# A four-layer network on one core: dense experts 512 wide, linear attention and the last stage in another order, routing and Exp in groups

## Time and profile before

| | before |
|---|---|
| time, median of 3 runs (range) | 5162.6 us (5162.58 to 5174.09) |
| the profiled execution's own time | 5173.64 us |
| its span | 5171.9 us |
| granted TensorE clock, mean | 0.946 |
| TensorE busy | 4497.5 us (87%), 36266 matmuls |
| VectorE busy | 3763.9 us (73%) |
| ScalarE busy | 3222.1 us (62%) |
| GpSimd busy | 2164.2 us (42%) |

### The profile page before, as it was taken

How to read it: one execution, slowest core, us unless ns; L and a number is a source line. 1 busy time by engine, 2 the same in 40 slices (tenths; PEclk the granted TensorE clock), 3 DMA queues, 4 the chain that set the end, 5 groups by cost and what they waited for, 6 DMA issues and landing times. The chain is left out here.

```text
span 5171.9 us, 91179 instructions
## 1 busy us (share of the span) xinstructions
PE 4497.5 (87%) x36266; PEld 2367.1 (46%) x36266; DVE 3763.9 (73%) x4573; ACT 3222.1 (62%) x4306; POOL 2164.2 (42%) x1131
## 2 busy tenths in 40 slices
PE   6999999999987998677878699868859988899998
PEld 3666666666755443111111244356634443333333
DVE  6888888888644776598898377757757756787777
ACT  3777777777833775377777477745527754444544
POOL 3888888888800232000000022234412224566665
PEclk7999999999998999599999799989979998999999
DMA  2111211111101110100000111000011103333333
GB/s 59 39 39 42 45 41 39 39 39 39 26 3 39 45 61 23 42 21 29 17 25 9 43 62 55 28 18 1 1 43 48 55 30 82 85 93 90 95 95 78
DMA packets 83156, 227.89 MB, mean 44 GB/s; under 512 B 18708, under 2 KB 23988, under 8 KB 79092
## 3 DMA queue, kind: packets, MB, share of 16 engines
q1 hardware_dynamic: 82767, 222.49, 15.4%
HBM read 160.12 MB, written 11.98 MB: 33 GB/s over the span
## 5 line engine op out<-in xcount | busy, mean ns | idle before, releaser
L527 POOL TENSOR_TENSOR a_prob_low<-a_prob_whole,a_prob_high 128x1024 f16<-128x1024 f32 x512 | 1084.8, 2131 | 276.8 <-ACT a_prob_high L417 276.8
L2263 DVE TENSOR_TENSOR e_low<-e_whole,e_high 128x1024 f16<-128x1024 f32 x400 | 696.5, 1763 | 284.5 <-ACT e_high L2221 284.5
L501 DVE TENSOR_REDUCE a_part_max<-a_top 128x2 f32<-128x1024 f32 x512 | 626.3, 1223 | 218.3 <-PE a_top L328 212.4
L414 ACT ACTIVATE a_prob_whole<-a_score 128x1024 f32<-128x1024 f32 x512 | 525.0, 1025 | 332.6 <-PE a_score L317 320.6
L778 ACT ACTIVATE a_prob<-a_score 128x512 f32<-128x512 f32 x1024 | 532.9, 604 | 259.4 <-PE a_score L722 259.4
L811 DVE TENSOR_REDUCE a_part_max<-a_side 128x2 f32<-128x1024 f32 x512 | 595.7, 1221 | 88.4 <-PE a_side L693 88.4
L2246 POOL TENSOR_TENSOR all_res_t<-all_res_t,e_gated 128x1024 f32<-128x1024 f32 x100 | 239.0, 2390 | 816.8 <-DVE e_gated L2272 816.8
L2218 ACT ACTIVATE e_whole<-e_hidden,e_bias 128x1024 f32<-128x1024 f32 x400 | 445.1, 1113 | 217.6 <-PE e_hidden L2169 130.7
L1920 POOL TENSOR_TENSOR m_scaled<-m_acted,m_gate 128x512 f32<-128x512 f32 x264 | 432.1, 1640 | 343.4 <-DVE m_acted L2047 255.9
L417 ACT ACTIVATE a_prob_high<-a_score 128x1024 f16<-128x1024 f32 x512 | 522.3, 1020 | 0.0
L316 PE MATMUL a_score<-a_qa,a_ka 128*128 128x256 f16 x2048 | 476.3, 273 | 0.0
(11 more groups left out here) (333 smaller groups left out, 10279.6 us busy)
## 6 DMA issues: line engine op xcount, KB each, us to landing
m_gate<-gates SPq DMA_DIRECT2D x264, 256.0 KB, 5.1
e_gate<-gates SPq DMA_DIRECT2D x25, 2048.0 KB, 7.2
a_ka<-a_nat_high_k SPq DMA_DIRECT2D x128, 128.0 KB, 2.4
e_w<-in_w_moe SPq DMA_DIRECT2D x25, 512.0 KB, 7.7
a_qa<-a_nat_high_q SPq DMA_DIRECT2D x64, 128.0 KB, 2.4
a_qa<-a_nat_low_q SPq DMA_DIRECT2D x64, 128.0 KB, 2.4
a_qb<-a_nat_high_q SPq DMA_DIRECT2D x64, 128.0 KB, 2.4
a_kb<-a_nat_low_k SPq DMA_DIRECT2D x64, 128.0 KB, 2.4
```

Of the source, the lines that this page charges most:

```text
L414: eng.activation(prob_whole[:, e % RING, :, :, :], score[:, e % 2, :, :, :], ACT.Exp, scale=scale)
L501: eng.tensor_reduce(part_max[:, i, c, :, qt % 4], top[:, :, :], AX.X, ALU.max).then_inc(max_done, 1)
L527: eng.tensor_tensor(prob_low[:, e % RING, :, :, :], prob_whole[:, e % RING, :, :, :], prob_high[:, e % RING, :, :, :], ALU.subtract).then_ ...
L2263: eng.tensor_tensor(low[:, s % HR, :], whole[:, s % 2, :], high[:, s % HR, :], ALU.subtract).then_inc(low_done, 1)
```

## The change

- Dense experts: W from 1024 to 512, so 32 steps a unit, a product of three matmuls, four hidden and four output banks (HB, OB), LAG 4, HR 8, SPLIT_AT 12: the same data in flight. ScalarE's, VectorE's and GpSimd's operations become 512 wide.
- Rope attention: the projections of batch 1 alone move 13 events ahead.
- Linear attention: another ORDER, for all engines.
- Last stage: START 24 to 12, PERIOD 35 to 34. VectorE and GpSimd take a step's part of it one slot later (UP_LAG 1), high and lows at HIGH_LAG 2 as before, the output at LAG 4; VectorE's addition is first in the slot after, mixing jobs last. ScalarE does high before Silu. The Exp jobs are split in two groups, slots 10 and 13; Sqrt from 45 to 36. Constants are padded with zeros to 128x128 tiles, and the pick matmuls accumulate. Routing is one chain per group of eight tiles, `weights(g)`; transposes go through `out` and `o_ps` in slots 2 to 5, ScalarE copies them, four stores with their own semaphores. The low half of x is made by GpSimd.

```diff
-                put(start + 1, "q", b + 1)
-                put(start + 3, "k", b + 1)
-                put(start + 9, "v", b + 1)
+                early = EV - 3 if b == 0 else 0
+                put(start + 1 - early, "q", b + 1)
+                put(start + 3 - early, "k", b + 1)
+                put(start + 9 - early, "v", b + 1)
...
-    ORDER = [("k0", 0), ("v0", 0), ("q0", 0), ("state", 1), ("ksum", 1), ("k1", 0), ("turn0", 2), ("v1", 0), ("fold", 1),
+    ORDER = [("k0", 0), ("state", 1), ("v0", 0), ("ksum", 1), ("q0", 0), ("turn0", 2), ("k1", 0), ("fold", 1), ("v1", 0),
              ("turn1", 2), ("q1", 0), ("out0", 2), ("out1", 2)]
...
-    PART_LAG, LAG, SPLIT_AT = 2, 4, 8
+    UP_LAG, HIGH_LAG, LAG, SPLIT_AT = 1, 2, 4, 8
     HB, AR, SR, HR = 2, 3, 4, 6
-    START, PERIOD = 24, 35
-    SLOTS = START + STEPS + LAG
+    START, PERIOD = 12, 34
+    SLOTS = START + STEPS + LAG + 1
     PAIR = 2 * BANK
-    GROUP_TILES = BANK // SMALL_EXPERTS
+    GROUP_TILES = PAIR // P
     BANKS = NT // GROUP_TILES
-    ROUTED = 1 + 2 * BANKS + 5
+    CHAIN = 7
...
-             "w0": 9, "w1": 9, "w2": 10, "w3": 10, "v0": 11, "k0": 12, "r0": 13, "v1": 14, "k1": 15, "r1": 16, "o0": 17,
-             "v2": 18, "k2": 19, "r2": 20, "o1": 21, "v3": 22, "k3": 23, "r3": 24, "o2": 25, "g": 26, "o3": 27,
+             "w0": 8, "w1": 9, "v0": 10, "w2": 11, "w3": 12, "k0": 13, "r0": 14, "v1": 15, "k1": 16, "r1": 17, "o0": 18,
+             "v2": 19, "k2": 20, "r2": 21, "o1": 22, "v3": 23, "k3": 24, "r3": 25, "o2": 26, "g": 27, "o3": 28,
              "mean": 30, "var": 33, "out": 63}
-    ACT_AT = {"low": 1, "low5": 2, "wt": 6, "ew0": 10, "ew1": 10, "ew2": 10, "ew3": 10,
-              "decay0": 10, "decay1": 10, "decay2": 10, "decay3": 10, "vs0": 12, "vs1": 15, "vs2": 19, "vs3": 23,
-              "gs": 27, "o": 28, "sq": 32, "std": 45}
+    ACT_AT = {"low": 1, "low5": 2, "wt": 6, "ew0": 10, "ew1": 10, "decay0": 10, "decay1": 10, "vs0": 11,
+              "ew2": 13, "ew3": 13, "decay2": 13, "decay3": 13, "vs1": 16, "vs2": 20, "vs3": 24,
+              "gs": 28, "o": 29, "sq": 32, "std": 36}
     DVE_AT = {"z": -1, "mixed1": 3, "mixed3": 4, "mixed2": 5, "mixed0": 7, "mixed4": 8,
-              "kv0": 13, "carry0": 13, "scan0": 13, "u0": 14, "rs0": 14, "kv1": 16, "carry1": 16, "scan1": 16, "u1": 17, "rs1": 17,
-              "kv2": 20, "carry2": 20, "scan2": 20, "u2": 21, "rs2": 21, "kv3": 24, "carry3": 24, "scan3": 24, "u3": 25, "rs3": 25,
-              "cen": 31, "eps": 34, "rstd": 47, "norm": 50, "affine": 50, "gated": 53, "res": 64}
+              "kv0": 14, "carry0": 14, "scan0": 14, "u0": 15, "rs0": 15, "kv1": 17, "carry1": 17, "scan1": 17, "u1": 18, "rs1": 18,
+              "kv2": 21, "carry2": 21, "scan2": 21, "u2": 22, "rs2": 22, "kv3": 25, "carry3": 25, "scan3": 25, "u3": 26, "rs3": 26,
+              "cen": 31, "eps": 34, "rstd": 43, "norm": 45, "affine": 45, "gated": 47, "res": 64}
     POOL_AT = {"delta": -2, "x1": 3, "x3": 4, "x2": 5, "x0": 7, "x4": 8}
-    LAST = {"std": 35, "rstd": 35, "norm": 36, "affine": 36, "gated": 36, "out": 37, "res": 38}
+    LAST = {"std": 35, "rstd": 36, "norm": 36, "affine": 36, "gated": 36, "out": 38, "res": 39}
...
+        shape = {"cols": [P, 20], "w_x1": [P, 2, P], "w_x2": [P, 5, P], "w_w1": [P, P], "w_w2": [P, GROUPS, P], "w_r": [P, GROUPS, P], "w_k": [P, GROUPS, P], "w_v": [P, GROUPS, P],
+                 "w_g": [P, P], "w_o": [P, P], "pick": [P, GROUPS, P], "blocks": [P, P]}
...
-                eng.wait_ge(turned_free, CH)
-                eng.dma_start(gates_d, gates_t[:, :]).then_inc(stored, 16)
-                eng.wait_ge(stored, 16)
+
+                def store(pair):
+                    eng.wait_ge(copied, 2 * (pair + 1))
+                    eng.dma_start(gates_d[:, pair * PAIR:(pair + 1) * PAIR], gates_t[:, pair % 2, :]).then_inc(stored[pair], 16)
+
+                for pair in range(2):
+                    store(pair)
                 for n in range(UNITS):
                     for pair in range(CH // 2):
                         g = n * (CH // 2) + pair
+                        if n == 0:
+                            eng.wait_ge(stored[pair], 16)
+                        if g == 1:
+                            store(2)
+                            store(3)
...
+                    eng.wait_ge(found, 1 + CHAIN * (g + 1))
+                    if i >= 2:
+                        eng.wait_ge(copied, i - 1)
                     for t in range(4):
-                        mm = eng.transpose(turned[0:EX, t * P:(t + 1) * P], gates[:, 4 * c + t, :], ident[:, :])
+                        mm = eng.transpose(turned[i % 2][0:EX, t * P:(t + 1) * P], gates[:, g % 2, i % 2 * 4 + t, :], ident[:, :])
                     mm.then_inc(turned_full, 1)
...
-                        eng.matmul(o_ps[32 * j:32 * j + 32, :], const["pick"][:, :], rs[:, j % 2, :], start=True, stop=True).then_inc(pe_done, 1)
+                            if c == 0:
+                                eng.wait_ge(copied, CH)
+                        eng.matmul(o_ps[:, :], const["pick"][:, j, :], rs[:, j % 2, :], start=j == 0, stop=j == GROUPS - 1).then_inc(pe_done, 1)
...
-                    if 9 <= slot < 9 + CH:
-                        turn(slot - 9)
+                    if 2 <= slot < 2 + BANKS:
+                        turn(2 * (slot - 2))
+                        turn(2 * (slot - 2) + 1)
...
+                    if slot == 10:
+                        for pair in range(CH // 2):
+                            eng.wait_ge(stored[pair], 16)
...
-                    if slot == 8:
+                    if 2 <= slot < 2 + BANKS:
+                        pair = slot - 2
+                        if pair >= 2:
+                            eng.wait_ge(stored[pair - 2], 16)
+                        for i in range(2):
+                            eng.wait_ge(turned_full, 2 * pair + i + 1)
+                            eng.activation(gates_t[:, pair % 2, i * BANK:(i + 1) * BANK], turned[i][0:EX, :], ACT.Copy).then_inc(copied, 1)
+                    if slot == 3:
                         split(0)
-                    if 11 <= slot < 11 + CH // 2:
-                        at = slice((slot - 11) * PAIR, (slot - 10) * PAIR)
+                    if 4 <= slot < 4 + CH // 2:
+                        at = slice((slot - 4) * PAIR, (slot - 3) * PAIR)
                         eng.activation(x_high[:, at], xn_t[:, at], ACT.Copy).then_inc(x_high_done, 1)
+                    s = step_at(slot, HIGH_LAG)
+                    if s >= 0:
+                        eng.wait_ge(scaled_done, s + 1)
+                        if s >= HR:
+                            eng.wait_ge(out_used, s - HR + 1)
+                        eng.activation(high[:, s % HR, :], scaled[:, s % SR, :], ACT.Copy).then_inc(high_done, 1)
                     s = step_at(slot, 0)
                     if s >= 0:
-                        if s == 0:
-                            eng.wait_ge(stored, 16)
                         eng.wait_ge(hidden_full, s + 1)
                         if s >= AR:
                             eng.wait_ge(scaled_done, s - AR + 1)
                         eng.activation(acted[:, s % AR, :], hidden[:, s % HB, :], ACT.Silu).then_inc(silu_done, 1)
                         if s % PER_UNIT == SPLIT_AT and s // PER_UNIT + 1 < UNITS:
                             split(s // PER_UNIT + 1)
-                    s = step_at(slot, PART_LAG)
-                    if s >= 0:
-                        eng.wait_ge(scaled_done, s + 1)
-                        if s >= HR:
-                            eng.wait_ge(out_used, s - HR + 1)
-                        eng.activation(high[:, s % HR, :], scaled[:, s % SR, :], ACT.Copy).then_inc(high_done, 1)
...
-                    for name, c in pool_jobs[slot]:
-                        mix(name, c)
-                    if slot == 9:
+                    if slot == 3:
                         split(0)
-                    s = step_at(slot, 0)
+                    if 4 <= slot < 4 + CH // 2:
+                        at = slice((slot - 4) * PAIR, (slot - 3) * PAIR)
+                        eng.wait_ge(x_high_done, slot - 3)
+                        eng.tensor_tensor(x_low[:, at], xn_t[:, at], x_high[:, at], ALU.subtract).then_inc(x_split, 1)
+                    s = step_at(slot, UP_LAG)
...
+                    for name, c in pool_jobs[slot]:
+                        mix(name, c)
...
+                def weights(g):
+                    r, tiles = g % 2, slice(g * GROUP_TILES, (g + 1) * GROUP_TILES)
                     eng.wait_ge(scored, g + 1)
-                    for t in range(g * GROUP_TILES, (g + 1) * GROUP_TILES):
-                        op = eng.max(best[:, t, :], score[:, t, :])
+                    for t in range(GROUP_TILES):
+                        op = eng.max(best[:, g * GROUP_TILES + t, :], score[:, g * GROUP_TILES + t, :])
                     then(op)
```

(45 more changed lines are left out.)

136 lines of the change are left out of this document (56 added, 80 removed).

## The result

| | before | after |
|---|---|---|
| median of the runs | 5167.4 us (4 runs, 5162.6 to 5174.1) | 5044.1 us (4 runs, 5035.9 to 5048.3) |
| ratio, 95% interval | | 0.9757 (0.9743 to 0.9772) |
| span of the profiled execution | 5171.9 us | 5046.1 us |
| granted clock, mean | 0.946 | 0.948 |

What follows compares the result with a forecast made beforehand. It took TensorE's matmuls, plus its waits for other engines and spells at the lower clock, as the bound. Gains of 64 + 42 + 8 + 91 = 205 us from a median of 5162.6 gave 4960 us, range 4905 to 5045.

Steps and rivals of the forecast that it cites:

- The chain against the lead: Dense experts: 512 wide, high and low take at most 3 us of a 5.2 us lead, so waits go; gain 64 us.
- Rival B: Dense experts stay bound by VectorE and GpSimd: gain 25 us instead of 64, total 5000 us; chance 0.12.
- my layout of what follows: Linear attention: hand-laid operations after ksum, giving a unit of 10.2 us and a gain of 42 us.
- The mechanism: Rope attention: batch 1's early f32 projections raise the clock sooner, near 2140 us, and it stays; gain 8 us.
- Last stage, start: Last stage: routing in four groups lets the first expert product come 24 us earlier, at 4306.4 us.
- Last stage, steady: Last stage from its first expert product: padding and fewer stalls, 67 us less.
- The drain: Last stage, behind the last step: 3 us, the same before and after the change.
- The padding: Last stage: full 128x128 tiles take away the 26 us that partial tiles add.
- the stalls: Last stage: 4.6 us a chunk for 11.5 before, and 3 at the tail, 40 us in all.
- the sentence that the addition: Last stage: VectorE's addition, leading its slot, comes 1.2 us sooner against a mean wait of 1.4; waits under 10 us.
- rival D: Last stage: the ring up, scaled, high, low binds; slower than before, 5310 us with 5 us delay everywhere; chance 0.02.
- Rival A: Last stage: ScalarE's table loads are not covered, about 48 us lost, total 5008 us; chance 0.22.

Runs made afterwards that it cites:

- run 7: Changed kernel with dense experts 512 wide but half the data and lead in flight, and rope projections of batch 1 at their old events: 5096.1 us.
- run 9: Changed kernel with experts 1024 wide, output 3 steps behind, split at step 9; old rope projection events; all eight Exp in one group: 5063.7 us.
- Run 8: Changed kernel with experts 1024 wide, output 3 steps behind, split at step 6; linear attention with q0 ahead of ksum: 5097.5 us.
- run 2: Changed kernel with high and low, and the output product, one slot later in the last stage: 5011.1 us, ratio 0.9689 to the kernel before.
- run 3: Changed kernel with VectorE's time-mixing jobs ahead of low in the last stage's slots: 5011.5 us, ratio 0.9692 to the kernel before.
- run 4: Changed kernel with the 15 padded f32 matmuls of a chunk on partial tiles again: 5051.0 us, ratio 0.9768 to the kernel before.
- run 6: Changed kernel with high and low a slot later, mixing jobs ahead of low, and the padded matmuls on partial tiles again: 5018.4 us, ratio 0.9697.
- run 1: Changed kernel with ScalarE doing Silu ahead of high in the last stage, as before the change: 5121.3 us, ratio 0.9902 to the kernel before.
- run 12: Changed kernel with VectorE's product with up and GpSimd's scaling in their own step's slot again (lag 0): 5129.0 us, ratio 0.9926.
- run 5: Changed kernel with high and low a slot later and mixing jobs ahead of low: 5006.9 us, ratio 0.9677 to the kernel before.

## Why the prediction was right, and where it was not

**Experts: right, 66.4 for 64**, and the stages 340, 378 and 339 for 338, 379 and 338 forecast. TensorE's wait for low fell from 46.0 to 4.0 us. That sum starts at a matmul's modelled end. Counted from start to start, the distances above 0.5 us, less 0.2158 each, fell from 67.0 to 5.3 us in the three stages, 62 of the 66. The chain against the lead was the reason: run 7 halves the lead, with the banks, and takes the gain away at the same width, and run 9 makes the lead longer and gives all but 7 us of it with the wide operations. Low beside GpSimd took up to 2.54 us, more than the 1.9 that I had, and the lead covered it. Rival B did not happen.

**Linear attention: 26.8 for 42.** The unit fell from 11.58 to 10.57 us, not to 10.2. TensorE's idle time ahead of ksum is 1.09, near the 1.0 laid out and down from 1.74, so the removed wait was the right one. What failed is my layout of what follows. VectorE's and ScalarE's rows of a unit of the changed kernel:

```profile
3556.65 1.48 DVE L1274 SCALAR_TENSOR_TENSOR a_q_s<-a_grown,a_clipped 128x512 f32<-128x512 f32 x1 [2.37 <-ACT a_clipped L1215]
3558.12 0.69 DVE L1274 SCALAR_TENSOR_TENSOR a_k_s<-a_grown,a_clipped 128x512 f32<-128x512 f32 x1
3558.92 1.93 DVE L1246 TENSOR_REDUCE a_k_part<-a_k_s 128x128 f32<-128x1024 f32 x1
```

```profile
3556.98 0.62 ACT L1214 ACTIVATE a_grown<-a_ring 128x512 f32<-128x512 f32 x1
3557.46 0.63 ACT L1215 ACTIVATE a_clipped<-a_ring 128x512 f32<-128x512 f32 x1
```

Q0's map took 1.48 beside GpSimd's product, not 0.7. But k1's map could not have begun sooner after a short one: ScalarE had its data ready at 3558.09, 0.03 us before it began, and so in 28 of 31 units. Two entries of the layout end late together, q0's map and ScalarE's pair for k1, which stands behind q0's pair and turn0's copy. From k0's map to k1's map it takes 5.56 us for 5.3 laid out, from there to the next k0's map 5.01 for 4.9. That is 12 of the 15 us; no run separates the two entries. The rest are mainly the batch ends: four units there took 0.3 to 2.3 us more than 10.57, 5.1 in all, for about 1 before. Run 8 moves q0 ahead, and the unit takes 10.29, with 2.1 us idle in VectorE for 2.4: k1's map then stands 1.31 us for ScalarE's pair and takes 1.46 itself, beside GpSimd's product, which I had not counted either.

**Rope attention: nothing for 8.** The mechanism set in, in part: the clock rose 67 us behind the first Exp for 80 before, and the 120th Exp came 114.4 us behind the first, for 119.7. In all nine kernels with the early events the rise comes at 59 to 67 us; in four of the other five at 80 or 81, in run 7 at 58. But the lead does not last even so far in all of them: the 120th Exp is at 123.8 and 123.9 us in runs 2 and 3, where the clock fell again soon after the rise. And the clock, full from 2197 to 2726 us in the kernel before, fell to the lower level at three other places in the changed kernel's stage, 41 us in all for 25 before, and the 5 us were gone. The fault was to price a rise of the clock as if what follows stayed fixed. The runs show the stage anywhere in 766 to 785 us with the same order of work.

**Last stage, start: 20.8 for 24.** Right; routing in groups put the first product 85.7 us behind the experts.

**Last stage, steady: 11.9 for 67.** Three terms. (The f32 matmuls between first and last step are 12 more than before, as forecast but for one behind the last step.) The drain: 24.4 us behind the last step's start for 18.6, where reciprocal, norm and gated stand ahead of up in the last slots, as the 3.87 us row shows. Behind that wait twelve f16 matmuls run at the lower clock, starting 0.43 us apart, for six before. I had it unchanged, so 6 us. The padding: its term, 26 us, is in the slots and even some 30 (slot 9, with the 64 rows of w1, has 0.30 in run 4, for the 0.15 that I took), but the time is worth 4 to 5 us here and 12 when VectorE is less late (runs 4 and 6). I had taken it as a gain of the path while all of its slots feed a chain that is waited for: the gain was given back as a wait. And the stalls, the mis-sized one: partial tiles and stalls together were to fall from 118 to 40, with 4.6 us a chunk and 3 at the tail; they fell from 116.0 to 88.0, 50 us less. With 26 to 30 of partial tiles in the 116.0, the stalls were some 86 to 90 before and are 88 now: what the new order took off them the padding put back (run 4 has 92.3 with its partial tiles in, so some 62 to 66 of stalls). The step of the prediction that failed is the sentence that the addition, now ahead in its slot, is sooner by up and low against a mean wait of 1.4, with waits under 10 us. They were 23.1; those for acted tiles, laid out at 0.5 us a chunk, were 20.0. It held VectorE's place in time as given, and only looked at the order inside a slot. In fact VectorE stands 76 us over five chunks at low, behind high, behind scaled, and what follows in its slot and in the next comes late; run 2, which takes 46 us of that wait away, takes 31 off the excess. I had this ring in the text, as rival D, priced it for all slots or none, found it not binding on the mean, and did not ask how much of it binds in the dense slots. What was right: the 1.8 us at slot 16, where k1 waits for the bank of rs0 (1.61 on the mean of eight), and the two groups of Exp, which pay (run 9).

**Rival A** (5008) was the nearest among those that were worked out, and its cause is not what happened: the Exp slots 10 to 13 cost 2.8 us a chunk for 6.6 before. Its page rule, the Trainium skill's "ScalarE: Activation LUTs", section "Rules for kernel authors", is to do all of one table set before switching. Run 9 does just that and its steps take 13.9 us more; here the length of one absence counted, not the number of 1.28 us loads. The other rule that was weighed, the Trainium skill's "TensorE: Matmul & The Clock Gate", section "LDWEIGHTS (loading the stationary operand)", that a load's time follows its columns and not its rows, is borne out by the rows of run 4: 108, 134 and 190 ns for 32, 64 and 128 columns of full height, 183 for 128 columns of 32 rows. The slot with the 32 columns was the longer one all the same.

**What the direction hangs on.** Runs 1 and 12 each undo one part of the new order and lose 77 and 85 us, more than the last stage gained in all. The order works only as a whole: what VectorE does in slot k must hang on nothing that TensorE makes in slot k. That holds for this order, with the addition in front; the kernel before has both couplings and the addition last, and an excess of 116.0, less than either run (167.1 and 177.8). Then runs 2, 3 and 5 show what was left: one slot more, or other work ahead of low. What makes up the last 48 us of excess (most of it in slots 10, 15, 3 and 0) was not tried.

## What to carry to other kernels

In a pipeline by slots, write for each engine what its first wait of a slot hangs on; a wait for something made in the same slot by the bottleneck can couple the two, and more lag in the other steps then helps little (12 us of 79 here). Here a slot of distance was worth 33 us, and shorter slots, by the padding, 4 to 12. A gain of a TensorE that is already waited for elsewhere, such as full tiles, is to be counted only as far as the engines behind can use it. And when buffers are halved in size to double their number, say whether it is the width or the time in flight that pays; a run of each can tell.

## What the runs showed of the hardware

An f32 matmul of 32 or 64 rows or columns among full ones makes its slot 0.23 to 0.30 us longer than a 128x128 one, though its weight load is as short (183 ns for 32 rows) or shorter (108 ns for 32 columns). A VectorE map of 128x512 (scalar_tensor_tensor, f32) takes 0.63 to 0.69 us alone and mostly 1.46 to 1.53 beside a GpSimd operation. In the unit shown, q0's map ended 0.54 us behind GpSimd's product (3555.22 for 2.36 us), in run 8 k1's map 0.56 behind it. TensorE's granted clock falls to the lower level at other places of the same attention stage after changes elsewhere in the program, so that a stage with the same order of work took 766 to 785 us, with 78 to 130 us of it at the lower level.
